# Alternating the convolutions and the mixes one by one on TensorE, with the mixes half a unit further behind

## The reference

```
x = x + conv1d(x, weight, groups=4, taps=9, pad=4) + (cond @ c_weight.T)[:, :, None] + bias[None, :, None]
h   = gelu(gelu(cond @ W0 + b0) @ W1 + b1)
att = softmax(h @ W2 + b2)                          # 128 x 8
agg_w = einsum("bk,koi->boi", att, weight8)         # one 64 x 64 matrix for each sample
x = x + einsum("boi,bih->boh", agg_w, x) + (att @ bias_k)[:, :, None]
```

## Time and profile before

| what | us |
|---|---|
| median of 3 timed runs | 248.84 |
| lowest and highest | 248.31, 249.13 |
| the profiled execution | 249.11 |
| its span | 247.3 |
| TensorE busy | 237.3 (96%) |
| VectorE busy | 220.3 (89%) |
| ScalarE busy | 126.6 (51%) |
| GpSimd busy | 10.4 (4%) |
| mean granted clock of TensorE | 0.985 |

### The profile page before, as it was taken

How to read it: one execution, slowest core, us unless ns; L and a number is a source line. 1 busy time by engine, 2 the same in 40 slices (tenths; PEclk the granted TensorE clock), 3 DMA queues, 4 the chain that set the end, 5 groups by cost and what they waited for, 6 DMA issues and landing times.

```text
span 247.3 us, 5763 instructions
## 1 busy us (share of the span) xinstructions
PE 237.3 (96%) x2162; PEld 103.9 (42%) x2162; DVE 220.3 (89%) x113; ACT 126.6 (51%) x208; POOL 10.4 (4%) x36
## 2 busy tenths in 40 slices
PE   6799999999999999999999999999999999999991
PEld 4643334344344444444444444444444444444530
DVE  1075899999999999999999999999999999999582
ACT  2457007374535456383645445373745446263772
POOL 1325000000000000000000000000000000000000
PEclk9689999999999999999999999999999999999999
DMA  7998566999999999999999999999999997444448
GB/s 189 307 326 240 152 125 191 258 312 365 357 322 268 359 263 383 249 380 238 334 294 292 327 256 378 247 388 239 362 273 322 298 281 293 170 170 172 171 184 328
DMA packets 28555, 68.39 MB, mean 277 GB/s; under 512 B 3184, under 2 KB 3568, under 8 KB 28544
## 3 DMA queue, kind: packets, MB, share of 16 engines
q1 hardware_dynamic: 19104, 50.98, 62.3%
q10 hardware_dynamic: 9440, 17.26, 26.5%
HBM read 34.67 MB, written 33.55 MB: 276 GB/s over the span
## 4 chain that ended last, share of the span: by engine, by line
PE 91%; DVE 3%; ACTq 2%; ACT 1%; issue 1%; DVEq 0%
PE yps L528 64%; PE zps L551 21%; PE yps L608 3%; DVE ynat L433 2%; ACTq L285 2%; PE yps L565 1%; PE zps L577 1%; DVE ycol L424 1%; PE yps L509 0%; PE yps L623 0%; PE yps L588 0%; ACT mixt L317 0%; DVE xin L498 0%; PE zps L588 0%; ACT L324 0%
## 5 line engine op out<-in xcount | busy, mean ns | idle before, releaser
L528 PE MATMUL yps<-xph,wraw 64*64 64x512 f32 x1512 | 169.0, 589 | 0.0
L303 ACT ACTIVATE zout<-zps,gamu 128x512 f32<-128x512 f32 x120 | 72.7, 688 | 95.3 <-PE zps L551 75.6
L528 PEld LDWEIGHTS yps<-xph,wraw 64*64 64x64 f32 x1512 | 67.5, 132 | 94.0 <-issue 94.0
L424 DVE STREAM_TRANSPOSE ycol<-yps 128x1024 f32<-128x1024 f32 x63 | 75.2, 1224 | 7.0 <-PE yps L528 5.4
L402 DVE STREAM_TRANSPOSE xph<-xin 128x4160 f32<-128x4160 f32 (+2 forms) x17 | 71.7, 4220 | 5.1 <-DMA xin<-in_x 5.1
L433 DVE STREAM_TRANSPOSE ynat<-ycol 128x4096 f32<-128x4096 f32 x15 | 66.7, 4446 | 1.1
L551 PE MATMUL zps<-ynat,mixv 64*64 64x512 f32 x480 | 57.8, 589 | 0.3 <-DVE ynat L433 0.3
L312 ACT ACTIVATE mixv<-mixt 64x256 f32 (+1 forms) x64 | 42.4, 663 | 1.4 <-ACT mixt L317 0.2
L551 PEld LDWEIGHTS zps<-ynat,mixv 64*64 64x64 f32 x480 | 21.6, 133 | 29.9 <-issue 29.6
L608 PE MATMUL yps<-zout 128*128 128x256 f32 x26 | 10.4, 566 | 1.3 <-POOL zout L243 1.3
L241 POOL COPY gamu<-gam 128x4 f32 (+1 forms) x16 | 2.9, 188 | 199.9 <-ACT zout L303 191.8
(11 more groups left out here) (56 smaller groups left out, 34.8 us busy)
## 6 DMA issues: line engine op xcount, KB each, us to landing
out<-zout SPq DMA_DIRECT2D x60, 512.0 KB, 6.2
xin<-in_x SPq DMA_DIRECT2D x64, 258.0 KB, 7.2
xin<-in_x ACTq DMA_DIRECT2D x64, 258.0 KB, 7.4
out<-xin SPq DMA_DIRECT2D x2, 512.0 KB, 2.7
out<-xin SPq DMA_DIRECT2D x4, 256.0 KB, 3.0
mlps<-in_mlp SPq DMA_DIRECT2D x1, 233.5 KB, 2.8
wraw<-in_conv_w ACTq DMA_DIRECT2D x1, 208.0 KB, 3.7
zout<-in_const_w SPq DMA_DIRECT2D x1, 160.0 KB, 9.3
```

What stands on the lines that cost most here:

```text
L303: nc.scalar.activation(zout[:, o].rearrange("p (i c j q) -> p c i j q", i=2, c=2, q=PH)[:, c], zps[:, at:at + BANK].rearrange("p (q i j) - ...
L424: nc.vector.transpose(ycol[:, :, :, :, :, g].rearrange("p i s j q c -> p (i s j) q c"), yps[:, 2 * BANK * (g % 2):2 * BANK * (g % 2) + 2 * ...
L528: last = nc.tensor.matmul(yps[C * c:C * c + C, at:at + BANK].rearrange("p (s f) -> p s f", s=S // 2), wsum[rows, b, g], xph[slot][rows, g, ...
```

## The change

Only TensorE's program is written in another order; no instruction is added or taken away, and the waits stand inside `conv` and `mix` as before. In a step of unit u the four convolutions of u and four mixes now alternate. The first two mixes are the second half of unit u − 2 (o = 2, 3), and the last two are the first half of unit u − 1 (o = 0, 1). Before, a step had two convolutions, two mixes, two convolutions, two mixes, all four mixes of unit u − 1.

```diff
             def step(u, slot):
 
                 conv(u, slot, 0)
+                mix(u - 2, slot, 2)
                 conv(u, slot, 1)
+                mix(u - 2, slot, 3)
+                conv(u, slot, 2)
                 mix(u - 1, 1 - slot, 0)
+                conv(u, slot, 3)
                 mix(u - 1, 1 - slot, 1)
-                conv(u, slot, 2)
-                conv(u, slot, 3)
-                mix(u - 1, 1 - slot, 2)
-                mix(u - 1, 1 - slot, 3)
...
             conv(1, 1, 0)
             conv(1, 1, 1)
+            conv(1, 1, 2)
             mix(0, 0, 0)
             pe.wait_ge(gam_made, 1)
+            conv(1, 1, 3)
             mix(0, 0, 1)
-            conv(1, 1, 2)
-            conv(1, 1, 3)
-            mix(0, 0, 2)
-            mix(0, 0, 3)
             step(2, 0)
...
             conv(NU - 1, 1, 0)
+            mix(NU - 3, 1, 2)
             conv(NU - 1, 1, 1)
+            mix(NU - 3, 1, 3)
             mix(NU - 2, 0, 0)
             mix(NU - 2, 0, 1)
```

## The result

The changed kernel takes 255.08 us in the median of 6 runs (253.95 to 256.02), against 248.74 us of the kernel before (6 runs, 248.02 to 249.13): a ratio of 1.0256, 95% interval 1.0234 to 1.0278. It is slower by 6.3 us. Its profiled execution took 255.06 us, with a span of 253.3 us, 6.0 above the 247.3 of before.

The account below looks back on a forecast made before the run. TensorE alone was taken to set the pace, VectorE following with 0.13 us to spare a unit. 1.30 + 3.8 + 0.86 + 1.2 = 7.2 us on the profiled 249.11 gave 256.3, so 256.0 for the median; range 252.0 to 259.2.

Parts of the forecast that it names:

- The likeliest case: Stall of TensorE for x of unit 3 and fall of the clock as forecast, 256.0 us; chance 0.45.
- Term 2: Load of x for unit 3, issued behind mix (0,1): lands late, convolution (3,0) stalls, 3.8 us lost.
- term 4: Granted clock falls behind the stall ahead of convolution (3,0): 1.2 us lost, bounds 0 and 3.4.
- The middle: Steady-state steps of the loop: VectorE's columns are in time by 0.7 us or more, cost 0.
- Term 1: First half of unit 1: convolution (1,2) waits for VectorE's columns (1,0), 1.30 us lost.
- Term 3: Last two steps: mix (14,1) waits for ScalarE to empty mix (13,3)'s bank pair, 0.86 us lost.
- The rival of the quicker load: ScalarE's and SyncE's loads take turns; unit 3's is whole in 9.3 us, stall 1.6, total 252.6 us; chance 0.14.
- The rival of the stall without the clock: Wait for x of unit 3 as forecast, clock stays at 1.00: 254.8 us; chance 0.27.

Follow-up runs that it names:

- experiment 1: Changed kernel with ScalarE's four DMAs of unit 3's x ahead of evacuate (0,0) instead of behind evacuate (0,1): 250.60 us, ratio 1.0073.
- Experiment 9: Changed kernel with the start in the old order, mixes (0,0) and (0,1) ahead of convolutions (1,2) and (1,3): 250.77 us, ratio 1.0083.
- experiment 4: Changed kernel with six extra matmuls between step 2 and the loop, while TensorE waits for x of unit 3: 253.82 us, ratio 1.0206.
- experiment 5: Changed kernel with mix (13,3) ahead of convolution (15,1) instead of behind it, in the tail: 252.93 us, ratio 1.0165.
- the changed kernel again: The changed kernel without further edits, run and profiled a second time: 254.78 us, ratio 1.0250.
- experiment 3: Kernel before with ScalarE's four DMAs of unit 3's x behind evacuate (0,3) instead of behind evacuate (0,1): 257.35 us, ratio 1.0341.
- experiment 6: Changed kernel with unit 3's x DMAs ahead of evacuate (0,0) and mix (13,3) ahead of convolution (15,1): 250.20 us, ratio 1.0055.
- Experiment 8: Changed kernel with SyncE's four DMAs of unit 4's x behind store (0,3) instead of ahead of store (0,2): 252.29 us, ratio 1.0150.

## Why the prediction was right

The forecast was 256.0 us in a range of 252.0 to 259.2; 255.08 was measured. The likeliest case is the one that came: a stall for x with a fall of the clock behind it, in both profiles of the changed kernel. That the sum is so close is partly luck. Term 2 came out 0.86 us too high and term 4 0.37 too low against the first profile (1.34 and 0.51 against the second), and the two errors cancel in part.

- *The middle at 0.* Shown: 49 quarters of a step fit to 0.02 us, and experiment 1 leaves no wait in it.
- *Term 1, 1.30.* Measured 1.35. VectorE's columns started at 35.07, 1.40 ahead of convolution (1,2), as its own order said. Experiment 9 adds what the prediction does not say: the term comes with the lag and moves when the order at this place is put back.
- *Term 2, 3.8.* Measured 2.94 and 2.46 in the two profiles, the term that was mis-sized most. The issue of the last DMA came 1.91 us behind the first where 2.1 was taken, and it landed in 8.7 (8.1 to 8.3 in the profiles of experiments 4 and 5 and of the changed kernel again) where 9.35 was taken. These two make up 0.84 of the 0.86, and both were in the bounds. The nearest row was the quietest group, 8.5. That ScalarE's issues hang on mix (0,1) and that the load had nothing to spare is shown from both sides by experiments 1 and 3.
- *Term 3, 0.86.* Measured 0.80; experiments 5 and 6 take it away.
- *Term 4, 1.2.* Measured 1.57 in one profile, 1.71 in the other, 0 in the profile of experiment 5 with a stall of 2.37. Experiment 4 takes the 1.57 away in the trace and 1.26 us off the median. By the rule of the Trainium skill, "TensorE: Matmul & The Clock Gate", section "Why this matters for your kernels", the term came to 1.7, which is nearer where the clock fell; it did not fall behind every stall.
- *The rival of the quicker load* had hold of something real and gave it too large a share. Experiment 8 shows that the two loads share the DMA engines, as "DMA: Bandwidth & Descriptors" of the Trainium skill has it, section "Queues, rings and completion order". By whose turn they do so, no run shows. Counted from its first DMA, the load was whole after 54.24 − 43.65 = 10.6 us, where the rival took 9.3 and the forecast 11.45. With SyncE's load out of the way the last DMA still takes 6.7 us. The stalls of 2.94 and 2.46 lie between the rival's 1.6 and the forecast's 3.8.
- *The rival of the stall without the clock* is what the profiles of experiments 4 and 5 look like, which are other kernels: 253.8 us and, without term 3, 252.9, where it said 254.8 with its larger stall. No profile of the changed kernel itself shows it.

Open: what decides whether the clock falls behind a stall of 2.4 us, and why the last landing was 11.6 us in experiment 3 and 8.7 here. One thing goes with it. Where the last DMA took long, ScalarE had begun to issue its next load well before that landing (6.9 us in the kernel before, where it took 11.3, and 10.4 us in experiment 3); in the changed kernel it was 54.24 − 50.51 = 3.7 us. No run tests whether this is the cause.

## What to carry to other kernels

When work is moved on one engine, follow every other engine whose program waits for the moved step, down to the DMAs that stand behind that wait; a load that names no wait in the profile may have no time to spare, and its landing set against its reader's start tells. An order that puts work off needs something to do in the meantime at the start and covers for it at the end; in a loop where it changes nothing, both ends still pay.

## What the runs showed of the hardware

A stall of 2.93 us that six matmuls filled, whose result nobody reads, was followed by a granted clock of 1.00; one of 2.94 us that was left idle was followed by 4.15 us at 0.62 on the mean, and a convolution that took 1.57 us longer. The kernel with more matmuls had the lower median, 253.82 against 255.08 us.

Near this length it was not certain: an idle stall of 2.37 us was followed by no fall of the clock, one of 2.46 us by a convolution that took 1.71 us longer.

The last of four DMAs of 258 KB from ScalarE's queue landed in 8.1 to 8.7 us with four equal ones from SyncE's queue beside it, and in 6.7 us when those were issued later.
